# A transformer layer with cross-attention on one core: the context is handed over with features first

## What is computed

```
for each b:
    h = x[b]
    n = layer_norm(h, ln1)                       # 256 features
    h = h + proj1(attention(n Wq1, n Wk1, n Wv1, causal))      # 16 heads of 16 features
    n = layer_norm(h, lnx)
    h = h + proj2(attention(n Wq2, ctx[b] Wk2, ctx[b] Wv2, bias=logits, causal+2))
    n = layer_norm(h, ln2)
    h = h + mlp(gelu(n Wfc))                     # 256 -> 1024 -> 256
```

## Time and profile before

| | us |
|---|---|
| median of 3 runs | 1320.84 (1320.83 to 1323.61) |
| profiled execution | 1324.19 |
| its span, first to last instruction | 1322.5 |
| TensorE busy | 1116.2 (84% of the span) |
| VectorE busy | 786.8 (59%) |
| ScalarE busy | 614.5 (46%) |
| GpSimd busy | 434.6 (33%) |

### The profile page before, as it was taken

How to read it: one execution, slowest core, us unless ns; L and a number is a source line. 1 busy time by engine, 2 the same in 40 slices (tenths; PEclk the granted TensorE clock), 3 DMA queues, 4 the chain that set the end, 5 groups by cost and what they waited for, 6 DMA issues and landing times.

```text
span 1322.5 us, 22082 instructions
## 1 busy us (share of the span) xinstructions
PE 1116.2 (84%) x7360; PEld 670.9 (51%) x7360; DVE 786.8 (59%) x1898; ACT 614.5 (46%) x1154; POOL 434.6 (33%) x805
## 2 busy tenths in 40 slices
PE   4394775888989999889989799899989999948967
PEld 2142442545455655556455555566456645534635
DVE  3471663576776677656767577667756677417513
ACT  1052242454664457444655357445744475505433
POOL 3041151243424342423524242434323243403220
PEclk9587796889999999999999899999989999988989
DMA  9406344908063543626081533626090800080000
GB/s 222 56 19 77 52 52 61 114 17 98 16 85 49 75 52 44 90 40 88 2 111 27 78 46 44 90 39 88 13 116 10 105 17 1 10 103 2 17 0 17
DMA packets 50391, 74.11 MB, mean 56 GB/s; under 512 B 6472, under 2 KB 24808, under 8 KB 50281
## 3 DMA queue, kind: packets, MB, share of 16 engines
q1 hardware_dynamic: 50281, 72.68, 40.0%
HBM read 17.45 MB, written 4.19 MB: 16 GB/s over the span
## 4 chain that ended last, share of the span: by engine, by line
PE 59%; issue 14%; DVE 10%; DMA 9%; ACT 6%; POOL 2%; SPq 1%; DVEq 0%; ACTq 0%; POOLq 0%
PE dense L515 14%; PE dense L521 12%; PE pv_out L588 10%; PE scores L574 8%; PE max_scores L556 7%; DVE row_max L789 5%; PE dense L509 3%; PE max_scores L559 3%; DMA q_stack_cross<-max_rows 3%; DMA q_stack_self<-parts_q 3%; DMA q_stack_self<-max_rows 2%; ACT probs L679 2%; DVE rest_k L822 1%; PE dense L611 1%; ACT inner L704 1%
## 5 line engine op out<-in xcount | busy, mean ns | idle before, releaser
L679 ACT ACTIVATE probs<-scores 128x512 f32<-128x512 f32 (+3 forms) x768 | 383.4, 529 | 455.7 <-PE scores L574 451.3
L789 DVE TENSOR_REDUCE row_max<-max_scores 128x1 f32<-128x512 f32 (+6 forms) x1024 | 445.6, 482 | 238.5 <-PE max_scores L559 233.9
L946 POOL TENSOR_SCALAR_AFFINE_SELECT probs<-probs 128x256 f32<-128x256 f32 x512 | 210.0, 430 | 464.1 <-ACT probs L679 463.3
L556 PE MATMUL max_scores<-k_stack_self,q_stack_self 96*128 96x512 bf16 (+3 forms) x512 | 148.7, 319 | 72.2 <-issue 56.0
L556 PE MATMUL max_scores<-k_stack_cross,q_stack_cross 99*128 99x512 bf16 (+3 forms) x512 | 145.8, 312 | 38.0 <-issue 31.7
L574 PE MATMUL scores<-q_stack_cross,k_stack_cross 101*128 101x512 bf16 (+3 forms) x512 | 135.4, 308 | 31.2 <-DMA q_stack_cross<-max_rows 19.6
L574 PE MATMUL scores<-q_stack_self,k_stack_self 98*128 98x512 bf16 (+3 forms) x512 | 137.1, 310 | 17.5 <-ACT probs L679 10.0
L521 PE MATMUL dense<-mlp_w,inner 128*128 128x256 f32 x512 | 127.7, 396 | 8.5 <-DVE rest_k L822 5.0
L515 PE MATMUL dense<-feat_b,fc_w 128*128 128x512 f32 x256 | 124.1, 610 | 3.0 <-ACT rest_k L713 1.1
L521 PEld LDWEIGHTS dense<-mlp_w,inner 128*128 128x128 f32 x512 | 97.5, 196 | 28.4 <-DVE rest_k L822 6.5
L556 PEld LDWEIGHTS max_scores<-k_stack_self,q_stack_self 96*128 96x128 bf16 x512 | 51.7, 101 | 108.9 <-issue 68.1
(11 more groups left out here) (95 smaller groups left out, 1500.7 us busy)
## 6 DMA issues: line engine op xcount, KB each, us to landing
q_stack_self<-parts_q SPq DMA_DIRECT2D x48, 256.0 KB, 9.5
k_stack_self<-parts_k SPq DMA_DIRECT2D x48, 256.0 KB, 15.5
q_stack_cross<-parts_q SPq DMA_DIRECT2D x48, 256.0 KB, 9.0
k_stack_cross<-parts_k SPq DMA_DIRECT2D x48, 256.0 KB, 12.7
x_in<-in_x SPq DMA_DIRECT2D x8, 512.0 KB, 10.7
x_in<-in_ctx SPq DMA_DIRECT2D x8, 512.0 KB, 10.4
hidden<-in_x SPq DMA_DIRECT2D x8, 512.0 KB, 13.4
out_y<-hidden SPq DMA_DIRECT2D x32, 128.0 KB, 1.7
```

What stands on the lines that cost most here:

```text
L556: pe.matmul(max_scores[:, bank, c0:c0 + W[q]], q_stack[at.kind][0:rows_, head, q * P:(q + 1) * P], k_stack[at.kind][0:rows_, head, 0:W[q]] ...
L679: nc.scalar.activation(probs[:, head % (2 * GH), c0:c0 + w], scores[:, part % EXP_BANKS, 0:w], ACT.Exp, scale=SCALE).then_inc(exp_done, 1)
L789: last = nc.vector.tensor_reduce(row_max[:, g % 2, c:c + 1], max_scores[:, part % MAX_BANKS, c0:c0 + W[q]], AX.X, ALU.max)
L946: nc.gpsimd.affine_select(out=v, in_=v, compare_op=ALU.is_ge, fill=0.0, base=q0 - kb * P + LAST[at.kind], pattern=[[0, 2], [1, P]], channe ...
```

## The change

The host hands over the context with features first (`np.swapaxes` of its last two axes), so one context is 256 rows of 2 KB instead of 512 rows of 1 KB. A new name `dC` in the table takes the place of `tc.0`: SP loads the context straight into `feat_a`, once the values `v1`, the last reader of what `feat_a` held, have been copied out. `k2` and `v2` wait for this transfer instead of the copies. `tc.1`, the transposes and ScalarE's copies are gone, and `x_in` holds only `x`: it is refilled with `x[b+1]` right behind `t1`.

```diff
@@ PLAN, slot Y
-    "Y": """0:dq1 9:dk1 0:u.6 0:y.2 0:f.7 0:dR 2:u.7 3:G.3 5:y.3 4:R1 8:v1.0 8:v1.1 11:tc.0 12:ta1.0
-            14:tc.1 14:ta1.1 16:p1.0 17:p1.1 20:k2.0 21:k2.1 22:ma.0 24:m.0 26:tx.0 27:tx.1 29:q2.0
+    "Y": """0:dq1 9:dk1 0:u.6 0:y.2 0:f.7 0:dR 2:u.7 3:G.3 5:y.3 4:R1 8:v1.0 8:v1.1 11:dC 12:ta1.0
+            14:ta1.1 16:p1.0 17:p1.1 20:k2.0 21:k2.1 22:ma.0 24:m.0 26:tx.0 27:tx.1 29:q2.0
@@ UNUSUAL, slot X of i=1
-    ("X", 1): """0:tc.0< 0:tc.1< 0:R1< 0:ta1.0< 2:ta1.1< 4:p1.0< 5:p1.1< 7:k2.0< 9:k2.1< 12:v2.0 14:v2.1
+    ("X", 1): """0:dC< 0:R1< 0:ta1.0< 2:ta1.1< 4:p1.0< 5:p1.1< 7:k2.0< 9:k2.1< 12:v2.0 14:v2.1
@@ SP
-                    if name == "tc" and part == HC - 1 and blike < NB - 1:
-
-                        wait(sp, turned["tc"], (b + 1) * HC)
-                        if blike + 2 < NB:
-                            sp.dma_start(x_in[:], x[b + 2].rearrange("(t p) h -> p t h", p=P)).then_inc(x_loaded, 16)
-                        else:
-                            sp.dma_start(x_in[:], ctx[NB - 1].rearrange("(t p) h -> p t h", p=P)).then_inc(ctx_loaded, 16)
-                    if name == "t1" and part == HC - 1:
+                    if name == "dC":
+
+                        wait(sp, v_ready["v1"], seen("v1"))
+                        sp.dma_start(feat_a[:], ctx[b].rearrange("(c p) t -> p c t", p=P)).then_inc(ctx_loaded, 16)
+                    if name == "t1" and part == HC - 1 and blike + 1 < NB:
 
                         wait(sp, turned["t1"], (b + 1) * HC)
-                        if blike > 0:
-                            sp.dma_start(x_in[:], ctx[b - 1].rearrange("(t p) h -> p t h", p=P)).then_inc(ctx_loaded, 16)
-                        else:
-                            sp.dma_start(x_in[:], x[1].rearrange("(t p) h -> p t h", p=P)).then_inc(x_loaded, 16)
+                        sp.dma_start(x_in[:], x[b + 1].rearrange("(t p) h -> p t h", p=P)).then_inc(x_loaded, 16)
@@ TensorE
-                    elif name == "tc":
-                        pe.wait_ge(ctx_loaded, (b + 1) * 16)
-                        last = turn(d, x_in, part)
...
                     elif name == "k2":
-                        pe.wait_ge(turned["tc"], (b + 1) * HC)
+                        pe.wait_ge(ctx_loaded, (b + 1) * 16)
                         last = by_feature(d, kv2_w, part * P, feat_a)
                     elif name in ("v1", "v2"):
-                        pe.wait_ge(turned["t1" if name == "v1" else "tc"], (b + 1) * HC)
+                        if name == "v1":
+                            pe.wait_ge(turned["t1"], (b + 1) * HC)
+                        else:
+                            pe.wait_ge(ctx_loaded, (b + 1) * 16)
@@ ScalarE
-                    elif name in ("tc", "ta1", "ta2"):
+                    elif name in ("ta1", "ta2"):
                         act.wait_ge(dense_made, made)
-                        nc.scalar.copy((feat_a if name == "tc" else feat_b)[:, part, :], d).then_inc(turned[name], 1)
+                        nc.scalar.copy(feat_b[:, part, :], d).then_inc(turned[name], 1)
@@ kernel
-        "in_x": x, "in_ctx": ctx_1024, "in_logits": L0_xattn_scorer_logits,
+        "in_x": x, "in_ctx": np.swapaxes(np.asarray(ctx_1024), 1, 2), "in_logits": L0_xattn_scorer_logits,
```

More of the change, by code:

```diff
@@ L191, in is_dense @@
 def is_dense(name):
-    return name not in ("M", "S", "PV", "R1", "R2", "R3", "L1", "u", "G", "y", "ma", "dR", "dq1", "dk1", "dq2", "dk2")
+    return name not in ("M", "S", "PV", "R1", "R2", "R3", "L1", "u", "G", "y", "ma", "dR", "dC", "dq1", "dk1", "dq2", "dk2")
 STARTED, BEFORE, _count = {}, {}, {}
@@ L342, in block_kernel @@
         attn_ready = sem("attn_ready")
-        turned = {n: sem(f"{n}_turned") for n in ("t1", "tc", "tx", "t2", "ta1", "ta2")}
+        turned = {n: sem(f"{n}_turned") for n in ("t1", "tx", "t2", "ta1", "ta2")}
         hi = {n: sem(f"{n}_hi") for n in stack_loaded}
```

## The result

The changed kernel takes 1333.93 us (median; 1327.29 to 1338.01), the kernel before 1321.29 us beside it: a ratio of 1.0089, 95% interval 1.0064 to 1.0113. By the medians it is slower by 12.6 us, by the ratio by 11.8, where 8 were forecast. The forecast's own band was 1324 to 1333 us, which 1333.93 just misses; the stated range of 1317 to 1336 holds it. The profiled execution took 1330.0 us, its span is 1328.3.

A forecast was written before the change was run, and what follows sets the result against it. TensorE's instruction order and transfers in a full, ordered queue were taken to bound the kernel. Waits at `k2` +8.6, b=0 -1.7, b=7 -0.9 and clock +2 gave +8.0 us, so 1329 us, range 1317 to 1336.

The forecast's parts named there:

- The bound: Whole kernel: TensorE's instruction order and the transfers it waits for set the time; the DMA queue is full and ordered.
- The landing: Slot Y, iterations 1 to 6: the context lands where the old `x_in` refill landed, at 698.6 for i=4.
- The first rival: Slot Y: the context lands long before `k2` and all removals count, 5.2 us won, 1315.6 us; chance 0.13.
- The waits, +8.6: At `k2`, iterations 1 to 6: TensorE waits for the context's landing, together +8.6 us, removed `tc.1` already included.
- The sign that I had named for it: TensorE, iterations 2 to 5: a stop of 2 to 3.5 us before `k2`, released by the transfer into `feat_a`.
- The clock, +2: Behind the new stops at `k2`, iterations 2 to 5: each costs 0 or 1.65 us more; 2 us taken.
- The transposes removed, -1.7 (b=0) and -0.9 (b=7): TensorE, first and last batch element: removing the context's transposes wins 1.7 us at low clock and 0.9 at full clock.
- The claim that `tc.1` is won only if nothing waits: TensorE, iterations 1 to 6: at best `tc.1` is won, 2.6 us, but a wait at `k2` ends with the transfer.
- The code's shift, taken as 0 of a range of 4 either way: Behind the loop's jump: moved code may shorten or lengthen TensorE's 4.17 us stop; zero taken, 4 us either side.
- time lost at the jump as a sign of being wrong: Loop's jump: the forecast is wrong if the lost time appears there instead of at `k2`.
- The sum: Whole kernel: waits +8.6, b=0 -1.7, b=7 -0.9 and clock +2 give +8.0 us.
- The third rival: Every new stop at `k2` also lowers the clock: +12.6 us, 1333.4, or 1337 with the loop's stop longer; chance 0.13.

The follow-up runs named there:

- e1: Changed kernel with the context's transfer issued ahead of the six key transfers in slot Y instead of behind them; 1323.24 us, ratio 1.0004 to the kernel before.
- e3: Changed kernel with one more 512 KB transfer, written to unused memory, issued right ahead of the context's; 1338.19 us, ratio 1.0130 to the kernel before.
- e2: Changed kernel with the context also loaded one slot earlier into `x_in`, which `k2` reads, `x_in` refilled behind `k2`; 1325.94 us, ratio 1.0025.
- e4: Changed kernel with idle identity transposes and 8-column copies put where the context's were; 1329.43 us, ratio 1.0064 to the kernel before.
- e10: e9 with the idle transposes and small copies of e4 at the context's old places; 1306.73 us, ratio 0.9891 to the kernel before.
- e6: Kernel before with the load of `hidden` moved from the slot's first beat to just ahead of the six key transfers; 1341.03 us, ratio 1.0141.
- e8: Kernel before with the load of `hidden` moved behind the row maxima, ahead of the keys, and GpSimd's add `R1` from beat 4 to 12; 1314.67 us, ratio 0.9950.
- e5: e1 with the load of `hidden` moved from the slot's first beat to behind the context's transfer; 1349.65 us, ratio 1.0237 to the kernel before.
- e9: e2 with the two moves of e8 (load of `hidden` and add `R1` later); 1325.31 us, ratio 1.0020 to the kernel before.

## Why the prediction was right, point by point

**The bound** (an ordered, full queue; TensorE's order and its transfers): right. e1 and e3 show it from both sides.

**The landing.** Right. It put the context 14.54 us behind S at i=4 (698.6 less 684.06); it landed at 14.6. From S to `k2` it wanted 14 to 14.6 us everywhere; the six are 14.02, 15.38, 16.11, 14.67, 14.56 and 14.12. At i=2 the transfer took 18.6 us and landed 15.2 behind S, which came a little earlier against the queue there; at i=3 it landed 15.6 behind S, and TensorE at the low clock came half a microsecond later still. The price from the Trainium skill (DMA: Bandwidth & Descriptors, "Anatomy of one DMA"), 3.2 us by that estimate, is that of a transfer alone. The trace has 17.7 us, and the measurement decides; the 3.6 to 3.9 us of e2's refills come near the price of the Trainium skill. The first rival falls with the 17.7 us.

**The waits, +8.6.** Right as a sum: S to `k2` is 9.2 to 10.2 us longer. By iteration the first profiles give +0.1, +3.6, +3.1, +3.2, +1.5 and -1.2 where I had 0, +2.2, +1.6, +3.1, +1.6 and +0.1. The sign that I had named for it, stops of 2 to 3.5 us at `k2` in the iterations 2 to 5, came at i=2 alone (3.05 us). In the iterations 3 to 5 the score matmul behind the stop for the row maxima took 0.61 us already; that stop had become longer by what `tc.0` had filled, and I had written that TensorE "only waits 0.44 longer" there and priced that at nothing. The landing hides this loss. e4, with `tc.0`'s place filled, has stops at `k2` in five iterations, of 0.2 to 3.1 us, and the same sum.

**The clock, +2.** Wrong. Behind `k2` I forecast a little over one drop. One came, at i=2: `k2` took 3.65 us, and from it to `dq2` 40.4 us instead of 38.7. But at i=1 the low clock that the kernel before had there is gone (0.90 before, 1.00 after), which I had not looked at, and `k2` to `dq2` is 2.1 us shorter in all.

**The transposes removed, -1.7 (b=0) and -0.9 (b=7).** About half of each is there. The long stretches of the table hide it: they differ by 1.6 and 1.7 us between two profiles of one kernel. Read from nearer events, from the score matmul behind the row maxima to `k2` of b=0, it is 10.26 and 10.25 us before, 9.38 and 9.36 after: 0.9 us won, not the 1.7 that the transposes took at the low clock. At b=7, from the score matmul between the places of `tc.0` and `tc.1` to `k2`, it is 10.05 in both profiles before and 9.61 in both after: 0.4 us. The claim that `tc.1` is won only if nothing waits agrees with e4, where eight idle transposes per iteration leave S to `k2` as it is.

**The code's shift, taken as 0 of a range of 4 either way.** This term was mis-sized too: +3.1 us, in both profiles of after. I had named time lost at the jump as a sign of being wrong; a quarter of the loss is there. All five profiles of kernels with transposes at these places before e10 (before twice, e4, e6, e8) have 158.7 to 158.8 us for the two jumps, e10 has 158.4; of the eight without, seven have 161.8 to 162.9, and e5 has 156.0 with VectorE's stop at one jump only 4.52 us long. The prediction looked at TensorE's stop alone and would have booked its loss as a gain; what counts is VectorE's, which outlasts it. Why TensorE's stop goes with the transposes was not tried further, nor were the small copies on ScalarE, which came and went with them in e4 and e10, tried apart.

**The sum.** +8.0 against +12.6. In the second profiles the waits give 0.6 more than forecast, the clock behind `k2` 4.1 less and the jump 3.1 more; the other rows add up to +2.6 where the removed transposes should have given -2.6, and no cause was found for that: single ones of these rows move by up to 1.9 us between two profiles of one kernel. So that the number came within 5 us owes something to luck, since the errors of clock and jump nearly cancel. The third rival had 12.6 us, the measured number, also by luck: the drops of the clock that it priced behind each new stop came at i=2 alone.

## What to carry to other kernels

Before an operand's transfer is given a new place, ask when its reader comes and what the queue holds until then: 0.44 us of work removed ahead of a wait is worth nothing, and a load that had a slot's time to land may cost its whole delay in a full queue. When a stop disappears, look for the next one along the same resource (here row maxima, `k2`, masks, `parts_k`) before the gain is booked. The order of the transfers was worth more than the work: moving one load and one add gave 8 us (e8), and the features-first context gave a gain beside it only in e10, where its reader did not hang on the crowded stretch and the idle transposes were kept. Where e10's gain over e8 comes from is open: from S to `dq2` it takes 313.5 us in its profile, e8 311.0.

## What the runs showed of the hardware that I had not expected

An engine that has less to do can end later: at i=4 the kernel with the idle transposes (e10) has a stop of 1.05 us behind `k2` and a granted clock of 0.98 in the 5 us around it, the one without (e9) 2.01 us and 0.74. VectorE stands 8.8 to 9.1 us with no releaser shown at 27 of the 28 jumps of the loop in the 14 profiles, whatever TensorE does, while TensorE's stop of 3.6 to 4.4 us there comes with the transposes and goes without them. And 512 KB more in the queue, written to memory, cost 0.7 us per iteration, less than the 1.2 us by which the old refill of the same size landed behind the keys.
